# Mask matmuls of two max banks together behind two score units, and PSUM banks split three and three

## The chip, the cores and the metric

The kernel runs on one core of a Trainium2 chip. The metric is the time of one execution in microseconds of device time, lower is better.

## The reference

One transformer layer on x of 16 sequences x 512 tokens x 128 channels: attention with 16 heads of 8 channels, a linear position bias and a causal mask, a residual with a layer norm, then eight experts of which each token takes two, a shared expert, and again a residual with a layer norm.

```python
q = (x @ q_w + q_b)   # 16 heads of 8
att = einsum('bhqd,bhkd->bhqk', q, k) / sqrt(8) + slope[h] * (j - i)
att = softmax(where(causal, att, -inf))
y = einsum('bhqk,bhkd->bhqd', att, v) @ o_w + o_b
x = layernorm(x + y)
x = layernorm(x + shared(x) + routed_top2(x))
```

## The kernel before

The first function, `attention`, does the attention and the first norm; the second, `experts`, the rest. Only the first is touched.

All of a sequence's q and k lie in stacks of bf16 rows: a float is split into three bf16 parts, whose products are summed by stacking them along the contraction, 48 rows, four more for the position bias, and then three rows for the negated row maxima and seven for the cut of blocks above the diagonal. Two heads lie above each other, one in partitions 0 to 63 and one in 64 to 127, so their matmuls use one half of TensorE's rows each.

Four heads make a quad (g = 0 to 3), and a sequence has four quads. The lower triangle of a quad's scores is packed into ten **units** of 512 columns, one PSUM bank each (`scores`, `unit`, L464). Before softmax the row maxima are needed. They come from a **max pass** one or two sequences ahead: 40 banks a sequence (`maxed`, `max_bank`, L441), each the scores without maxima, plus a mask matmul (L461) that adds the causal mask by multiplying an identity of 128 rows with a constant. The mask matmul is 128 columns wide in banks 0 to 3 of ten, 256 in 4 to 7, 384 in 8 and 9. VectorE reduces a bank to its maxima (`take_max`, L724, L732) and frees it by `max_taken`. Max bank n of a group of ten is issued right behind unit n of some quad (`MAX_AT`: quad 0 carries max 10 to 19, quad 1 20 to 29, quad 2 30 to 39, quad 3 0 to 9 of a later sequence), and its head is the neighbour (m ^ 1) of the unit's, so it lies in the other half of the rows and both run side by side.

After each unit: ScalarE takes the exponential (L562, `exp_done` frees the score bank), GpSimd zeroes above the diagonal (L602), and a quad later four matmul groups `pv0` to `pv3` (`weighted`, L482, L493) multiply the probabilities with v in 32-column strips of TensorE, in PSUM bank `pv`; ScalarE copies the result to `yraw` after `pv3` (L517).

Between them stand **jobs**, each a short pipeline through TensorE (all in the single PSUM bank `misc`, in fixed order, see `ready`), ScalarE, VectorE and GpSimd: `xt`, `q`, `k`, `qr`, `kr` (transposed input, q and k and their bf16 parts for the sequence two ahead), `y0` to `y3`, `v`, `yn`, `o`, `ln`, `x1t`, `lg` (normalisation, output projection, layer norm and router logits of the sequence before), `m`, `mr` (row maxima of the next sequence, split in three parts; SyncE then writes them into the stack by six DMAs, L379, which unit 0 and unit 1 of the next sequence wait for). `qr`, `kr`, `ln` and `mr` have no part on TensorE.

The order is one list, `plan(g)` (L164), which every engine walks in its own program, each taking the items that have a part for it. An engine works strictly in that order, so whatever waits holds all behind it. Before, the list is built from fractions of a quad and comes out as follows (max numbers shown from 0):

```
g0: u0 max0 xt u1 max1 pv0 u2 max2 q u3 max3 u4 max4 k pv1 u5 max5 u6 max6 qr pv2 u7 max7 pv3 u8 max8 kr u9 max9
g1: u0 max0 y0 u1 max1 pv0 u2 max2 y1 u3 max3 u4 max4 y2 pv1 u5 max5 u6 max6 y3 pv2 u7 max7 pv3 u8 max8 v u9 max9
g2: u0 max0 u1 max1 yn pv0 u2 max2 u3 max3 o u4 max4 pv1 u5 max5 u6 max6 ln pv2 u7 max7 pv3 u8 max8 x1t u9 max9
g3: u0 max0 u1 max1 m pv0 u2 max2 u3 max3 mr u4 max4 pv1 u5 max5 u6 max6 pv2 u7 max7 pv3 u8 max8 lg u9 max9
```

PSUM has eight banks: two for `scores` (SB), four for `maxed` (MB), `pv` and `misc`. A unit waits for the exponential of the unit SB before it, a max matmul for the reduction of the one MB before it.

Of the kernel before, what the change touches and what calls it, by code (L numbers as in the profile page):

```python
# [12 lines left out]
ACT = mybir.ActivationFunctionType  # L13
# [10 lines left out]
SB, MB = 2, 4  # L24
# [71 lines left out]
def max_stage(n):  # L96

    return 2 if n < 10 else 1
# [65 lines left out]
def plan(g):  # L164

    score = "unit0 unit1 pv0 unit2 unit3 unit4 pv1 unit5 unit6 pv2 unit7 pv3 unit8 unit9".split()
    jobs = list(JOBS[g])
    keyed, units = [], 0
    for x in score:
        if x.startswith("unit"):  # L170
            keyed += [(units / 10, 2, x), (units / 10, 3, f"max{MAX_AT[g] + units}")]
            units += 1
        else:
            keyed.append((units / 10, 1, x))
    early = {"m": 0.2, "mr": 0.35} if g == 3 else {}
    keyed += [(early.get(x, (n + 0.5) / len(jobs)), 0, x) for n, x in enumerate(jobs)]
    in_order = []
    for at, rank, x in sorted(keyed, key=lambda item: (-(-item[0] * 10 // 1), item[1])):
        in_order.append(x)
    return in_order  # L180
# [38 lines left out]
def attention(nc, io, dram, keep):  # L219

    with ExitStack() as ctx:
# [80 lines left out]
        with nc.Block() as block:  # L302
# [84 lines left out]
            def _(pe):  # L387
# [53 lines left out]
                def max_bank(st, n):  # L441
# [11 lines left out]
                    bank = maxed[n % MB]  # L453
                    q, ks = qstack[st.stack(off)], kstack[st.stack(off)]
                    blocks = max_blocks(n)
                    for h, i, col in blocks:
                        rows, slot = rows_of(h, MAX_ROW)
                        pe.matmul(bank[:, col:col + (i + 1) * P], q[rows, slot, i * P:(i + 1) * P],  # L458
                                  ks[rows, slot, 0:(i + 1) * P], start=True, stop=False, skip_group_check=True)
                    at, mask = ((3 * P, slice(0, P)), (2 * P, slice(0, 2 * P)), (P, slice(P, T)))[n % 10 // QUAD]  # L460
# [3 lines left out]
                def unit(st, g, u):  # L464
# [7 lines left out]
                    for hh in range(QUAD):  # L472
                        for kt in range(QT):
                            at, col, width = segment(hh, kt)
                            if at == u:
                                rows, slot = rows_of(g * QUAD + hh, ROWS)
                                last = pe.matmul(scores[n % SB][:, col:col + width],  # L477
# [21 lines left out]
                def body(st):  # L499
                    for g in range(NQUAD):  # L500
                        off, pg = (0, g - 1) if g else (-1, NQUAD - 1)
                        for item in plan(g):
# [4 lines left out]
                            elif item.startswith("max") and st.has(max_stage(int(item[3:]))):  # L507
                                max_bank(st, int(item[3:]))
                            elif item in READERS and st.has(STAGE[item]):
                                job(st, item)  # L510
# [4 lines left out]
            def _(act):  # L515
# [36 lines left out]
                def body(st):  # L552
                    for g in range(NQUAD):
                        off, pg = (0, g - 1) if g else (-1, NQUAD - 1)
                        for item in plan(g):
                            if item.startswith("unit") and st.has(0):
                                u = int(item[4:])
                                act.wait_ge(S["unit_ready"], st.at(0, SEQ_UNITS, UNITS * g + u + 1))
                                if u == 0 and (g >= 2 or not st.first(0)):
# [3 lines left out]
                                               scores[(UNITS * g + u) % SB][:], ACT.Exp).then_inc(S["exp_done"], 1)  # L563
# [67 lines left out]
            def _(dve):  # L631
# [92 lines left out]
                def take_max(st, n):  # L724
# [7 lines left out]
                    dve.tensor_reduce(out.rearrange("p a b -> p (a b)"), maxed[n % MB][:].rearrange("p (j t) -> p j t", t=P),  # L732
# [654 lines left out]
```

## Time and profile before

| | |
|---|---|
| time, median of three runs | 1538.52 us (1532.29 to 1545.63) |
| the profiled execution | 1540.48 us, span 1538.4 us |
| TensorE (PE) busy | 1215.7 us, 79% of the span, 9059 instructions |
| VectorE (DVE) | 857.5 us, 56% |
| ScalarE (ACT) | 771.2 us, 50% |
| GpSimd (POOL) | 609.4 us, 40% |
| mask matmuls (L461) | 640, 179.8 us busy; 151.4 us of idle time before their weight loads |
| mean granted TensorE clock | 0.889 |

Times count from the span's start. "Busy" of an engine is the union of its instructions; a row's idle time and the name behind the arrow say how long the engine stood before it and what ended that. PEld is TensorE's weight loading, which overlaps PE. In a timeline, equal instructions that follow each other are merged into one row with their count.

### The profile page before, as it was taken

Reading aid. Unit: us, or ns where it says so; the run is one execution under the profiler, and the core shown is the slowest. Engines: PE = TensorE matmul, PEld = TensorE weight load, DVE = VectorE, ACT = ScalarE, POOL = GpSimd, SP = SyncE. Lnnn points to the kernel's source line nnn. Section 1 sums busy time; section 2 is a strip of 40 time slices with the busy share of each in tenths; the row PEclk is TensorE's granted clock in tenths of the full one; section 3 lists DMA queues with packets and bytes.
Section 4 is the critical chain, followed back from the end, with each engine's and each line's share of the span. In section 5 each row is a group of like instructions: output and inputs, shape, how many; then the busy total and the mean of one; then the engine's idle time right before and its main releaser. Section 6 shows DMA issues by size and latency. Waiting matters only on the chain. (4 is left out here: it accounts for less than half of the span.)

```text
span 1538.4 us, 29410 instructions
## 1 busy us (share of the span) xinstructions
PE 1215.7 (79%) x9059; PEld 753.4 (49%) x9060; DVE 857.5 (56%) x2153; ACT 771.2 (50%) x1659; POOL 609.4 (40%) x1064
## 2 busy tenths in 40 slices
PE   1989999999999999999864101169799989999865
PEld 0223333333333333333223100069799979999755
DVE  1768888888788888887115000024433325564556
ACT  1036666666666666666621000036566656666332
POOL 0024444444444444444322777600000015552677
PEclk9969999999899999999855555579899989999898
DMA  6433333444323334441106111100022223332222
GB/s 94 59 47 67 67 63 63 61 70 72 73 43 65 65 64 65 63 65 25 32 0 160 55 53 53 48 19 23 28 60 60 60 59 99 103 103 80 70 78 74
DMA packets 147325, 96.41 MB, mean 63 GB/s; under 512 B 21777, under 2 KB 142929, under 8 KB 147026
## 3 DMA queue, kind: packets, MB, share of 16 engines
q1 hardware_dynamic: 131682, 73.19, 24.7%
q0 software_dynamic: 8192, 16.79, 3.8%
q10 hardware_dynamic: 7344, 5.08, 1.4%
q8 instruction: 58, 0.95, 0.3%
q14 instruction: 49, 0.40, 0.1%
HBM read 33.39 MB, written 31.46 MB: 42 GB/s over the span
## 5 line engine op out<-in xcount | busy, mean ns | idle before, releaser
L562 ACT ACTIVATE probs<-scores 128x512 f32<-128x512 f32 x640 | 363.4, 594 | 176.4 <-PE scores L477 176.1
L602 POOL TENSOR_SCALAR_AFFINE_SELECT probs<-probs 128x256 f32<-128x256 f32 (+1 forms) x640 | 241.5, 384 | 360.9 <-ACT probs L562 353.5
L458 PE MATMUL maxed<-kstack,qstack 52*128 52x512 bf16 (+3 forms) x1024 | 261.5, 317 | 30.9 <-DMA kstack<-parts 27.9
L477 PE MATMUL scores<-qstack,kstack 64*128 64x128 bf16 (+3 forms) x1024 | 250.4, 311 | 30.3 <-ACT probs L562 17.9
L1024 DVE TENSOR_TENSOR e_hid<-e_gate,e_up_ps 128x352 f32<-128x352 f32 x208 | 108.2, 520 | 276.0 <-ACT e_gate L1282 184.6
L1205 PE MATMUL e_gate_ps<-e_w_in,e_xT 128*128 (+1 forms) x624 | 164.3, 373 | 91.1 <-issue 73.4
L732 DVE TENSOR_REDUCE maxA<-maxed 128x4 f32<-128x512 f32 x256 | 170.1, 685 | 83.6 <-PE maxed L461 79.9
L493 PE MATMUL pv<-probs,vaug 128*32 128x512 f32 (+3 forms) x2048 | 203.2, 472 | 0.0
L1282 ACT ACTIVATE e_gate<-e_gate_ps 128x352 f32<-128x352 f32 x208 | 96.7, 465 | 201.9 <-PE e_gate_ps L1205 79.2
L732 DVE TENSOR_REDUCE maxB<-maxed 128x4 f32<-128x512 f32 x256 | 168.5, 683 | 28.0 <-PE maxed L461 26.3
L477 PEld LDWEIGHTS scores<-qstack,kstack 64*128 64x128 bf16 x1024 | 65.4, 94 | 234.5 <-ACT probs L562 146.8
L461 PE MATMUL maxed<-causal,identb 128*128 128x128 bf16 (+2 forms) x640 | 179.8, 281 | 0.0
L1323 POOL DMA_INDIRECT e_raw_down<-y_sorted,e_place_best x64 | 63.3, 989 | 289.7 <-DMA y_sorted<-e_raw_down 277.8
L1205 PEld LDWEIGHTS e_gate_ps<-e_w_in,e_xT 128*128 128x128 f32 x624 | 101.6, 198 | 108.0 <-issue 85.1
L1205 PE MATMUL e_up_ps<-e_w_in,e_xT 128*128 (+1 forms) x624 | 141.0, 336 | 0.0
L461 PEld LDWEIGHTS maxed<-causal,identb 128*128 128x128 bf16 x640 | 61.6, 96 | 151.4 <-issue 151.4
L1223 PE MATMUL e_h_ps<-e_ident,e_hid 128*128 128x128 f32 x624 | 106.7, 281 | 21.7 <-issue 15.8
L1234 PE MATMUL e_y_ps<-e_w_down,e_running 128*128 (+3 forms) x624 | 89.7, 281 | 34.7 <-issue 20.5
L1234 PE MATMUL e_y_ps<-e_w_down,e_counts 128*128 (+3 forms) x624 | 89.5, 280 | 32.5 <-issue 31.3
L1205 PEld LDWEIGHTS e_up_ps<-e_w_in,e_xT 128*128 128x128 f32 x624 | 112.7, 200 | 0.0
L1285 ACT ACTIVATE e_xT<-e_x_ps 128x128 fp32r<-128x128 f32 x208 | 57.8, 278 | 92.6 <-remote 31.2
L732 DVE TENSOR_REDUCE maxC<-maxed 128x4 f32<-128x512 f32 x128 | 87.6, 686 | 26.3 <-PE maxed L461 24.6
(158 smaller groups left out, 1737.0 us busy)
## 6 DMA issues: line engine op xcount, KB each, us to landing
qstack<-parts SPq DMA_DIRECT2D x192, 64.0 KB
kstack<-parts SPq DMA_DIRECT2D x192, 64.0 KB
x_sorted<-zeros SPq DMA_DIRECT2D x32, 288.0 KB, 5.3
e_xs<-x_sorted SPq DMA_DIRECT2D x144, 64.0 KB
y_sorted<-e_raw_down SPq DMA_DIRECT2D x144, 64.0 KB, 1.6
xin<-in_x SPq DMA_DIRECT2D x16, 256.0 KB, 3.2
xres<-in_x SPq DMA_DIRECT2D x16, 256.0 KB, 3.3
e_xs<-x_all SPq DMA_DIRECT2D x64, 64.0 KB
```

Of the source, the lines that this page charges most:

```text
L458: pe.matmul(bank[:, col:col + (i + 1) * P], q[rows, slot, i * P:(i + 1) * P], ks[rows, slot, 0:(i + 1) * P], start=True, stop=False, skip_ ...
L461: pe.matmul(bank[:, at:T], identb[:], causal[:, mask], start=False, stop=True, skip_group_check=True).then_inc(S["max_ready"], 1)
L477: last = pe.matmul(scores[n % SB][:, col:col + width], ks[rows, slot, kt * P:(kt + 1) * P], q[rows, slot, kt * P:T], start=True, stop=True)
L493: last = pe.matmul(pv[hh * VW:(hh + 1) * VW, kt * P:T], vaug[st.par(off)][:, kt, g * QUAD + hh, :], probs[g % 2][:, at * T + col:at * T + ...
L562: act.activation(probs[g % 2][:, u * T:(u + 1) * T], scores[(UNITS * g + u) % SB][:], ACT.Exp).then_inc(S["exp_done"], 1)
L602: pool.affine_select(out=view, in_=view, compare_op=ALU.is_ge, fill=0.0, base=0, pattern=pattern, channel_multiplier=-1).then_inc(S["maske ...
L732: dve.tensor_reduce(out.rearrange("p a b -> p (a b)"), maxed[n % MB][:].rearrange("p (j t) -> p j t", t=P), AX.X, ALU.max).then_inc(S["max ...
L1024: dve.tensor_tensor(hid[k][:, 0:F], gate[k][:], up_ps[k][:, 0:F], ALU.mult).then_inc(S["hid_done"], 1)
L1205: last = pe.matmul(bank[:, 0:F], xT[k][:, x_part, :], w_in[:, e, w, w_part, :].rearrange("p a f -> p (a f)"), start=n == 0, stop=n == 2)
L1223: last = pe.transpose(h_ps[:, j * P:(j + 1) * P], hid[k][:, j * P:(j + 1) * P], ident[:])
L1234: last = pe.matmul(y_ps[:, 0:C], hT[k][0:fw, j * P:(j + 1) * P], w_down[0:fw, e, j, :].rearrange("p a c -> p (a c)"), start=j == 0, stop=j ...
L1282: act.activation(gate[k][:], gate_ps[k][:, 0:F], ACT.Silu).then_inc(S["silu_done"], 1)
```

## The change

SB and MB go from 2 and 4 to 3 and 3. The mask matmul leaves `max_bank` for a function of its own, `mask_bank`, and a plan item `mask<n>` issues it for max banks n and n+1. `plan` becomes an explicit loop over pairs of units: unit, max, unit, max, the two masks, a `pv`, a job. As 40 is no multiple of 3, the bank's number now comes from a count over all sequences.

```diff
-SB, MB = 2, 4
+SB, MB = 3, 3
 def plan(g):
...
+    in_order = []
     jobs = list(JOBS[g])
+    after = {0: jobs[0:1], 1: jobs[1:2], 2: jobs[2:3], 3: jobs[3:4], 4: jobs[4:]}
+    if g == 2:
+        after = {0: ["yn"], 1: ["o"], 2: [], 3: ["ln"], 4: ["x1t"]}
+    elif g == 3:
+        after = {0: ["m"], 1: ["mr"], 2: [], 3: ["lg"], 4: []}
+    for n in range(UNITS // 2):
+        for u in (2 * n, 2 * n + 1):
+            in_order += [f"unit{u}", f"max{MAX_AT[g] + u}"]
+        in_order.append(f"mask{MAX_AT[g] + 2 * n}")
+        if n < QUAD:
+            in_order.append(f"pv{n}")
+        in_order += after[n]
     return in_order
 def max_bank(st, n):
-                    bank = maxed[n % MB]
+                    bank = maxed[st.at(off, MAXB, n) % MB]
+                def mask_bank(st, n):
+                    bank = maxed[st.at(max_stage(n), MAXB, n) % MB]
                     at, mask = ((3 * P, slice(0, P)), (2 * P, slice(0, 2 * P)), (P, slice(P, T)))[n % 10 // QUAD]
                     pe.matmul(bank[:, at:T], identb[:], causal[:, mask], start=False, stop=True,
                               skip_group_check=True).then_inc(S["max_ready"], 1)
 def unit(st, g, u):
-                                last = pe.matmul(scores[n % SB][:, col:col + width],
+                                last = pe.matmul(scores[st.at(0, SEQ_UNITS, n) % SB][:, col:col + width],
 def body(st):
+                            elif item.startswith("mask") and st.has(max_stage(int(item[4:]))):
+                                mask_bank(st, int(item[4:]))
+                                mask_bank(st, int(item[4:]) + 1)
```

ScalarE's exponential and VectorE's reduction take their bank's number in the same way. The new lists, with max numbers from 0 and `masks` for two mask matmuls:

```
g0: u0 max0 u1 max1 masks pv0 xt u2 max2 u3 max3 masks pv1 q u4 max4 u5 max5 masks pv2 k u6 max6 u7 max7 masks pv3 qr u8 max8 u9 max9 masks kr
g1: the same with y0, y1, y2, y3, v
g2: the same with yn, o, nothing, ln, x1t
g3: the same with m, mr, nothing, lg, nothing
```

## Rows read from the trace of the kernel before

**Rows 1.** Busy by stretch: from:to, length, PE, PEld, DVE, ACT, POOL, clock, DMA share.
```profile
91.00:742.00 651.00, 607.06 (x5191) 244.94 (x5190) 523.65 (x1106) 426.97 (x788) 299.75 (x685) 0.98 0.37 61
```

**Rows 2.** Timeline of ScalarE: start, length, what; the copies after `pv3`.
```profile
380.14 0.60 ACT L517 ACTIVATE yraw<-pv 128x512 f32<-128x512 f32 x1 [0.22 <-PE pv L493]
393.20 0.60 ACT L517 ACTIVATE yraw<-pv 128x512 f32<-128x512 f32 x1 [0.22 <-PE pv L493]
...
437.76 0.60 ACT L517 ACTIVATE yraw<-pv 128x512 f32<-128x512 f32 x1 [0.23 <-PE pv L493]
...
480.87 0.60 ACT L517 ACTIVATE yraw<-pv 128x512 f32<-128x512 f32 x1 [0.22 <-PE pv L493]
```

**Rows 3.** Waits of one period, 439.6 to 482.7: total us, times, longest.
```profile
PE misc L392 <- DVE x_tiles L717: 1.0, 1, 1.0
...
PE scores L477 <- ACT probs L562: 0.8, 2, 0.5
...
PE scores L477 <- DVE maxA L732: 0.5, 1, 0.5
```

**Rows 4.** Timeline of TensorE in quad 0 (L392 `xt`, L405 `q`).
```profile
440.00 0.61 PE L392 MATMUL misc<-ident,xin 128*128 128x128 f32 x4
440.54 0.39 PE L477 MATMUL scores<-qstack,kstack 64*128 64x512 bf16 x1
...
440.86 0.23 PE L461 MATMUL maxed<-causal,identb 128*128 128x128 bf16 x1
441.02 1.07 PE L493 MATMUL pv<-probs,vaug 128*32 128x512 f32 x8
...
442.34 0.23 PE L461 MATMUL maxed<-causal,identb 128*128 128x128 bf16 x1
442.40 1.08 PE L405 MATMUL misc<-xT,wq 128*128 128x512 f32 x2
...
443.74 0.23 PE L461 MATMUL maxed<-causal,identb 128*128 128x128 bf16 x1
443.90 0.33 PE L477 MATMUL scores<-qstack,kstack 64*128 64x384 bf16 x1
...
444.07 0.22 PE L477 MATMUL scores<-qstack,kstack 64*128 64x128 bf16 x1
```

**Rows 5.** Timeline of TensorE, the same quad: `pv1` and `pv2`.
```profile
445.38 0.85 PE L493 MATMUL pv<-probs,vaug 128*32 128x384 f32 x8
...
447.25 0.43 PE L493 MATMUL pv<-probs,vaug 128*32 128x128 f32 x8
```

**Rows 6.** Timeline of VectorE and ScalarE around `k` (its TensorE part ends 445.38).
```profile
445.49 0.75 DVE L652 TENSOR_SCALAR k_whole<-misc,kb 128x512 f32<-128x512 f32 x1
...
446.28 0.63 ACT L517 ACTIVATE parts<-k_whole 128x512 bf16<-128x512 f32 x1 [0.37 <-DVE k_whole L652]
...
446.81 1.07 ACT L562 ACTIVATE probs<-scores 128x512 f32<-128x512 f32 x2
```

**Rows 7.** Timeline of VectorE in quad 2: job `o`, reductions, `ln`.
```profile
466.54 0.69 DVE L705 TENSOR_TENSOR x_tiles<-misc,xres 128x512 f32<-128x512 f32 x1
...
468.57 1.85 DVE L732 TENSOR_REDUCE maxB<-maxed 128x4 f32<-128x512 f32 x3
470.35 1.49 DVE L717 TENSOR_SCALAR x_tiles<-x_tiles,mean_var,rstd 128x128 f32<-128x128 f32 x4
```

**Rows 8.** Timeline around the DMAs of the row maxima (L379) and unit 1.
```profile
434.80 3.76 SPq L379 DMA_DIRECT2D qstack<-mparts  x6
...
477.57 0.31 DVE L683 TENSOR_TENSOR mparts<-mrest,mparts 64x128 bf16<-64x128 f32 x1
...
477.91 4.53 SPq L379 DMA_DIRECT2D qstack<-mparts  x6
...
483.81 0.09 PEld L477 LDWEIGHTS scores<-qstack,kstack 64*128 64x128 bf16 x1 [0.34 <-DMA qstack<-mparts]
```

**Rows 9.** Busy by stretch, columns as in the first group: a stretch at falling clock.
```profile
380.00:390.00 10.00, 8.65 (x52) 2.42 (x48) 7.67 (x19) 5.47 (x11) 4.16 (x12) 0.70 0.05 14
```

More of the change, by code:

```diff
@@ L164, in plan @@
 def plan(g):
-    score = "unit0 unit1 pv0 unit2 unit3 unit4 pv1 unit5 unit6 pv2 unit7 pv3 unit8 unit9".split()
+    in_order = []
     jobs = list(JOBS[g])
[L168 to L179, printed above, removed]
+    after = {0: jobs[0:1], 1: jobs[1:2], 2: jobs[2:3], 3: jobs[3:4], 4: jobs[4:]}
[10 more added lines that the diff above has]
+        in_order += after[n]
     return in_order
@@ L452, in max_bank @@
                         pe.wait_ge(S["max_taken"], st.at(off, MAXB, n - MB + 1))
-                    bank = maxed[n % MB]
+                    bank = maxed[st.at(off, MAXB, n) % MB]
                     q, ks = qstack[st.stack(off)], kstack[st.stack(off)]
-                    blocks = max_blocks(n)
-                    for h, i, col in blocks:
+                    for h, i, col in max_blocks(n):
                         rows, slot = rows_of(h, MAX_ROW)
@@ L562, in body @@
                                 act.activation(probs[g % 2][:, u * T:(u + 1) * T],
-                                               scores[(UNITS * g + u) % SB][:], ACT.Exp).then_inc(S["exp_done"], 1)
+                                               scores[st.at(0, SEQ_UNITS, UNITS * g + u) % SB][:], ACT.Exp).then_inc(S["exp_done"], 1)
                             elif item == "pv3" and st.has(off):
@@ L731, in take_max @@
                         out = maxC[:, h:h + 2, :]
-                    dve.tensor_reduce(out.rearrange("p a b -> p (a b)"), maxed[n % MB][:].rearrange("p (j t) -> p j t", t=P),
+                    dve.tensor_reduce(out.rearrange("p a b -> p (a b)"), maxed[st.at(max_stage(n), MAXB, n) % MB][:].rearrange("p (j t) -> p j t", t=P),
                                       AX.X, ALU.max).then_inc(S["max_taken"], 1)
```

## Prediction

> **What bounds the kernel now.** I read the busy time by stretch first [rows 1]. From 91 to 742 us all sixteen sequences pass through attention; TensorE is busy 607 of 651 us (93%), VectorE 524 (80%), ScalarE 427 (66%). Nothing behind attention uses the plan or the banks, so only this stretch can change, and I read it for one sequence. The copies of `yraw` after `pv3` repeat exactly: from the one at 437.76 to the one four quads on, at 480.87, is 43.1 us [rows 2]; some 14.5 such periods carry the whole max pass (the last sequence has none left to do). The list of waits of one period [rows 3] shows what TensorE misses: 1.0 us for the normalised tile before `x1t`, 0.8 us for exponentials, 0.5 us for a reduction; with 93% busy that is about 3 us of 43.1 in all. So TensorE is the bound, by a small margin.
>
> Its own timeline [rows 4] shows what it spends. Below, a time from one row to the next is the difference of starts. A score and a max matmul of 512 columns run side by side (on the two halves of the rows). From 440.54 to the mask at 440.86 is 0.32 us, though 512 columns at the granted 2.4 GHz take 0.21: about 0.10 us more before a full-height matmul may start. From a 128-column mask (0.05 us of columns) to the next unit is 0.16 (443.74 to 443.90), to `pv` 0.16, but to `q`, which is full-height too, only 0.06. So a change of shape (half-height rows, full height, 32-column strips) costs about 0.10 us each time, and a repeat costs none: the second segment of a unit follows after 0.17 us, the length of its 384-column predecessor (443.90 to 444.07).
>
> The Trainium skill, TensorEngine Tiling (Array Packing), Key Properties, says that changing the tiling mode, not just the tile, drains TensorE; that is the gap seen above. The Trainium skill, TensorE: Matmul & The Clock Gate, Part 3, The mechanism, adds that a weight load overlaps running matmuls only where the row group differs; by that rule a second unit behind the first would show its load of 0.09 us [rows 8] and 20 pairs would lose 1.8 us of the 2.9 saved below. The 0.17 us spacing on one row group speaks against it here.
>
> **Part 1: masks in pairs.** Counting changes of shape through the old plan gives 24 a quad (10 from a unit into a mask, 10 into a unit, 4 into `pv`; jobs stand behind masks and cost none), 96 a sequence. The new one has 5 + 5 + 4 and one for each job that now stands behind a `pv` (3, 4, 2 and 2): 17, 18, 16 and 16, 67 in all. That is 29 fewer at 0.10, so 2.9 us of TensorE time per sequence, 42 us in 14.5. If nothing else became late this would be the gain. A step that no row shows is `pv` straight into a full-height job (11 a sequence): between 0 and 0.2 us (twice the dearest change seen), taken as 0.1 like the others. Unit after unit is also unseen: between 0.22 (columns alone, as within a unit) and 0.32 (with a drain); I take 0.22.
>
> **Part 2: later masks, three max banks, later jobs.** A max bank 2k+1 now needs the reduction of 2k-2, the first of the pair just before; with four banks there was one more in between. A job waits behind its `pv`. I follow one sequence in five legs, each from its latest chain. u is a unit, g0 to g3 the quads.
>
> Leg A, g0 u1 to the end of `k`: TensorE alone. Units 0.32 + 0.54 + 0.55, mask pairs 0.23 + 0.23 + 0.33 (0.07 or 0.11 for the first, 0.16 or 0.21 for the second), `pv0` 1.00, `pv1` 0.78, `pv2` 0.36 [rows 4, 5] (a row's duration overlaps its follower by 0.07, which is taken off), `xt` 0.54, `q` and `k` 1.02 each. Sum 6.9.
>
> Leg B, end of `k` to g1 u1: ScalarE. After `k` VectorE starts 0.11 later and takes 0.75; ScalarE's `k` copy 0.05 later, its follower 0.54 after that; two exponentials 1.07 [rows 6]; `yraw` copy 0.5; the `qr` copy, now behind it, 0.54; the exponential of unit 8 0.6, and 0.1 back to TensorE, where u1, three banks on, waits for it. Sum 4.2. TensorE's own work there is 2.7 (four units 1.1, masks 0.33 and 0.44, `pv3` 0.57, u0 0.22), so it stands 1.5 us even with three score banks; before, the exponentials cost it 0.8 [rows 3].
>
> Leg C, g1 u1 to the end of `o` in g2: TensorE again. Fourteen units in pairs, their masks, two `pv0` and two `pv1`, one `pv2`, one `pv3` (0.57, midway between its neighbours), five transpose jobs at 0.54 like `xt`, `v` and `o` 1.0 each (estimates from `q`). Sum 14.8. VectorE has 14 reductions at 0.60 there (their pace when they queue, three in 1.85 [rows 7]), 8.4 us, and jobs under 3 us: hidden.
>
> Leg D, end of `o` to g3 u0: VectorE. The `o` job (add, statistics) runs from 466.54 to 468.57, 2.03 us [rows 7]; behind it now stand four reductions (max 34 to 37) in place of three, 0.60 each, then `ln` 1.49, then `x1t` 0.54: with 0.1 to 0.2 at each hand-over 6.9 us, 0.6 of it new. TensorE reaches max 37 after 1.46 (u4 and u5 0.55, masks 0.33, `pv2` 0.36, u6 0.22), but the reduction of max 34, queued behind the `o` job, ends at 2.8: it waits 1.4 us there, and the masks of 36 and 37, `pv3` and u8 are late behind it; then `x1t` waits 1.3 us for `ln`. TensorE's savings of this leg go entirely into these two waits.
>
> Leg E, g3 u0 to g0 u1: the DMA of the row maxima. `m` now follows `pv0`: 0.54 + 0.23 + 1.00 + 0.20 = 2.0; the next pair's masks stand at 2.5, two reductions follow, and the `mr` job starts at 4.0 after u0. From its start to the unit that reads the result the trace has 477.57 to 483.81, 6.2 us, with a wait for the DMA already shown [rows 8]; there the six issues take 4.53, elsewhere 3.76, which makes 5.5. So u1 comes 9.5 to 10.2 after g3 u0; 9.8 taken. TensorE alone would be there after 8.3 (ten units 2.7, masks 1.6, the four `pv` 2.7, `m` and `lg` 1.1, u0 0.2).
>
> Sum: 6.9 + 4.2 + 14.8 + 6.9 + 9.8 = 42.6 us, against 43.1. Of 2.9 us saved some 0.5 is left; the rest becomes waiting.
>
> The other moves are hidden: ScalarE's, GpSimd's and SyncE's parts of `q` and `k` (24 stack DMAs) come up to two units later, but their stack is first read in g3, two quads on; GpSimd is busy 300 of 651 us [rows 1], and `pv` needs its selects a quad later.
>
> **Score banks 2 to 3** show in leg B: u9 and the next u0 may stand three exponentials ahead instead of two. They cost nothing but the max bank they take.
>
> **Sum.** 14.5 periods times 0.45 is 6.5 us. The start (max pass alone, 42 to 91 us) and the last sequence have the same chains of jobs; I take zero, give or take 3. Against that one more stretch at half clock: between the copies at 380.14 and 393.20 a quad took 13.1 us [rows 2] at a mean clock of 0.70 over ten of them [rows 9], where a quarter of the period is 10.8; TensorE's idle time grows from 3 to about 6 us a sequence, so I add 1. The profiled execution took 1540.5 us around a span of 1538.4; that gives 1535, and since it stood 2 above the median of the three runs (1538.5), 1533.
>
> **Rivals.**
>
> *The waits dissolve.* Where TensorE runs ahead, VectorE and ScalarE get their work earlier and may catch up; if leg E's DMA wait or leg B's exponential wait (1.5 us each) is absorbed, a period is 41.1: 1511; both, 39.6: 1490. For it: 2.9 us is a count on rows. Against: each leg's chain consists of durations, not of queues. From 0.7 us absorbed per period on it decides. Chance 0.28, around 1510.
>
> *The clock falls.* The new idle time is bunched (1.5 us before g1 u1, 1.4 and 1.3 in leg D). In the profile it fell without one long gap [rows 9]. The price is 13.1 less 10.8, 2.3 us; in every second sequence that gives 17 us, 1549, in each one 33 us, 1565. From about nine sequences on it ends slower. Chance 0.13. The Trainium skill, TensorE: Matmul & The Clock Gate, "A second HAM failure mode: psum-queue depth-cycling", tells of just this, micro-idle pieces at bank turns that make the clock oscillate; the trace agrees, with 0.70 in that stretch.
>
> *The pairs do not save.* If unit after unit costs 0.32, legs A and C grow by 0.1 for each of 11 pairs, 1.1 us: 1549. If `pv` into a job costs 0.2 as well, 9 of these add 0.9: 1562. Against: the repeat within a unit is free. Chance 0.14.
>
> **How the numbers follow.** Forecast 0.45, dissolve 0.28, clock 0.13, no saving 0.14. About 1% is what a measurement of this kernel tells from no change, 1523 to 1554. Faster: 0.28. Slower: the clock 0.13 and 0.09 of the last, 0.22. Same: the rest, 0.50. The range 1504 to 1562 leaves out both waits dissolved (below) and the clock falling in every sequence (above).
>
> **What would show it.** The idle time ahead of the masks' weight loads falls by about half. The period stands at 42.6 instead of 43.1. Score matmuls wait for the DMA of the maxima in nearly every sequence, about 1.5 us. Max matmul 37 waits for a reduction, `x1t` for `ln` about 1.3 us; the exponential before g1 u1 is waited for 1.5 us. A period at or under 41.4 would show legs B or E wrong; one above 43.6, the unit spacing or the clock.

## The result and the profile after

| | before | changed |
|---|---|---|
| median of 14 runs each | 1539.85 us (1531.42 to 1546.67) | 1520.21 us (1506.05 to 1527.88) |
| ratio, 95% interval | | 0.986 (0.9836 to 0.9883) |
| profiled execution, span | 1540.48, 1538.4 | 1506.05, 1504.0 |
| last copy of `yraw` (end of attention) | 789.10 | 758.93 |

The changed kernel is 1.4% faster. The forecast was 1533 us, with "no change" (1523 to 1554) as the likeliest class. The time lies in the range, 12.8 us below the forecast, but just under the 1523 that the prediction set as the edge of "no change", and the interval of the ratio leaves out 1. The profiled execution is the fastest of its 14, 14 us under their median, so terms read from it are compared with a second profile of each kernel below. Of all executions of this case two count as slow and stand in no ratio: one of the single masks (2546.56 us) and one of the jobs ahead of `pv` (1367.67).

Most lines moved down by three to six: scores are L480, max matmuls L457, masks L464, `pv` L496, exponentials L568, reductions L738, the copies to `yraw` L523, `ln` L723.

Busy by stretch, columns as in [rows 1], changed kernel, over the sequences that carry a max pass:

```profile
91.00:680.00 589.00, 533.97 (x4844) 221.12 (x4844) 494.21 (x1039) 383.58 (x735) 278.56 (x636) 0.99 0.40 66
```

TensorE is busy 91%, VectorE 84%. In the kernel before the same instructions take 91 to 698 us, and the shares are 94% and 82% ([rows 1] runs on to 742 us, into quads without max pass). TensorE lost work and VectorE came closer to it. The period, by the copies to `yraw` as in [rows 2] (timeline of ScalarE, changed kernel):

```profile
382.63 0.60 ACT L523 ACTIVATE yraw<-pv 128x512 f32<-128x512 f32 x1 [0.23 <-PE pv L496]
394.95 0.60 ACT L523 ACTIVATE yraw<-pv 128x512 f32<-128x512 f32 x1
404.35 0.60 ACT L523 ACTIVATE yraw<-pv 128x512 f32<-128x512 f32 x1
415.85 0.60 ACT L523 ACTIVATE yraw<-pv 128x512 f32<-128x512 f32 x1 [1.47 <-PE pv L496]
424.84 0.60 ACT L523 ACTIVATE yraw<-pv 128x512 f32<-128x512 f32 x1 [0.23 <-PE pv L496]
```

From 382.63 to 424.84 it is 42.2 us, where 43.1 was before and 42.6 forecast. What TensorE waits for in it (waits of 384.9 to 427.1; columns as in [rows 3]):

```profile
PE scores L480 <- ACT probs L568: 1.1, 2, 0.8
PE misc L392 <- DVE x_tiles L723: 1.0, 1, 1.0
PE maxed L457 <- DVE maxB L738: 1.0, 1, 1.0
PE scores L480 <- DMA qstack<-mparts: 0.7, 1, 0.7
```

These are the four waits that the prediction named, each at its place, and each smaller than forecast: 0.8 us before g1 u1 (the larger of the two in the first row) where it had 1.5, 1.0 for 1.3, 1.0 for 1.4, and 0.7 for 1.5. On TensorE's timeline of the same period:

```profile
385.57 0.39 PE L480 MATMUL scores<-qstack,kstack 64*128 64x512 bf16 x1 [0.71 <-DMA qstack<-mparts]
...
387.69 0.39 PE L480 MATMUL scores<-qstack,kstack 64*128 64x512 bf16 x1
387.70 0.60 PE L457 MATMUL maxed<-kstack,qstack 52*128 52x512 bf16 x2
387.92 0.38 PE L480 MATMUL scores<-qstack,kstack 64*128 64x512 bf16 x1
388.23 0.29 PE L464 MATMUL maxed<-causal,identb 128*128 128x128 bf16 x2
388.45 0.85 PE L496 MATMUL pv<-probs,vaug 128*32 128x384 f32 x8
389.23 1.12 PE L405 MATMUL misc<-xT,wq 128*128 128x512 f32 x2
...
392.57 0.33 PE L480 MATMUL scores<-qstack,kstack 64*128 64x384 bf16 x1
...
396.61 0.39 PE L480 MATMUL scores<-qstack,kstack 64*128 64x512 bf16 x1 [0.83 <-ACT probs L568]
...
414.50 0.39 PE L457 MATMUL maxed<-kstack,qstack 52*128 52x384 bf16 x2 [1.01 <-DVE maxB L738]
...
417.79 0.63 PE L392 MATMUL misc<-ident,x_tiles 128*128 128x128 f32 x4 [1.02 <-DVE x_tiles L723]
```

Unit follows unit after 387.92 − 387.69 = 0.23 us, the columns alone (so in five of the six pairs of 512 columns of this period in which no wait stands; the sixth has 0.33). The pair of masks starts 0.31 behind the second unit, and `pv1` stands 0.22 behind it. From `pv1` to `q` it is 0.78, what the prediction took for `pv1` ahead of a unit, so a `pv` into a job is as dear as one into a unit. A pair does save TensorE its changes of shape. In the sum it is less than was counted: from copy to copy TensorE is busy 40.4 of 43.1 us before (437.76 to 480.87) and 38.4 of 42.2 now (382.63 to 424.84), 2.0 us less where the count has 2.9, and its idle time grew from 2.7 to 3.8. The idle time ahead of the masks' weight loads fell, in 100 to 680 us, from 118.2 (534 recorded) to 74.0 us (552): 37% less, not the half that was forecast (weight loads of the changed kernel, 100 to 680 us: busy, mean ns of one, then idle and its cause):

```profile
L464 PEld LDWEIGHTS maxed<-causal,identb 128*128 128x128 bf16 x552 | 31.4, 97 | 74.0 <-issue 74.0
```

**Where the 32 us between the profiles lie.** A second profile of each kernel, on one chip, gives spans of 1538.5 and 1506.6. Divided by the copies to `yraw`, the second pair and in brackets the first:

| stretch | before | changed | less |
|---|---|---|---|
| up to the copy in g1 of the second sequence | 155.2 (153.5) | 147.6 (148.5) | 7.6 (5.0) |
| the twelve periods from there | 525.9 (523.9) | 514.2 (511.9) | 11.7 (12.0) |
| two quads more | 20.7 (20.7) | 20.5 (20.5) | 0.2 (0.2) |
| the last nine quads | 89.7 (91.0) | 76.3 (78.0) | 13.4 (13.0) |

Of the twelve periods' gain 12 x 0.9 = 10.8 is the period. Quads that stand above the others, at a low clock or behind a late DMA, come on top and nearly cancel: before they are five in the second pair (11.91, 13.07, 11.86, 11.86 and 11.85 us where the others take 10.4), 8.6 us in all, in the changed kernel chiefly three (13.86, 13.82 and 16.02 against 12.32), 7.6 us in all. Of the last nine quads it is chiefly the last five, in which nothing of the max pass runs any more, that gain: 50.9 us before and 39.1 changed (50.5 and 39.3). Behind attention the second pair is equal, 747.0 and 748.0. So some 11 of the 32 us are the period, and more than half of the gain came from the first sequence and from the end of attention. The max pass alone (42 to 91 us), ahead of the first sequence, gained nothing: ScalarE's first `xT` copy behind it comes at 93.67 us before and 93.63 changed (93.05 and 94.45 in the first pair). In the first sequence the granted clock is 0.68 from 93 to 116 us before and 0.80 from 93 to 110 changed; why it stays low for less time no run here takes apart.

Busy by stretch of the last five quads before (cut at the copies to `yraw`; after the length PE, PEld, DVE, ACT, POOL, clock, DMA share):

```profile
738.60:750.50 11.90, 9.28 (x58) 2.60 (x58) 0.19 (x1) 6.17 (x12) 3.95 (x11) 0.66 0.33 76
750.50:761.10 10.60, 9.73 (x65) 3.48 (x62) 2.19 (x8) 6.09 (x11) 4.54 (x11) 0.74 0.00 0
761.10:769.30 8.20, 7.07 (x62) 2.86 (x60) 1.94 (x9) 6.64 (x14) 3.25 (x9) 1.00 0.12 35
769.30:781.80 12.50, 9.03 (x53) 2.05 (x52) 1.50 (x4) 6.59 (x12) 5.83 (x16) 0.65 0.00 0
781.80:789.10 7.30, 7.23 (x44) 3.29 (x42) 0.19 (x1) 1.70 (x3) 2.18 (x4) 0.50 0.00 0
```

and changed:

```profile
719.60:730.60 11.00, 8.39 (x59) 2.36 (x58) 0.19 (x1) 5.95 (x13) 3.65 (x11) 0.69 0.35 84
730.60:738.10 7.50, 6.81 (x61) 2.82 (x60) 1.64 (x6) 5.74 (x13) 4.85 (x12) 1.00 0.00 0
738.10:745.70 7.60, 7.12 (x66) 2.96 (x64) 2.49 (x11) 6.07 (x14) 2.62 (x9) 1.00 0.04 11
745.70:755.50 9.80, 6.96 (x53) 2.07 (x52) 1.49 (x4) 6.20 (x14) 6.07 (x16) 0.83 0.07 21
755.50:758.90 3.40, 3.37 (x42) 1.53 (x42) 0.19 (x1) 1.70 (x4) 2.15 (x5) 1.00 0.00 0
```

The clock column shows the difference. Without max pass TensorE has only ten units, `pv` and jobs a quad. Before, it stood for an exponential six times (3.9 us in 740 to 789), and its clock was 0.50 to 0.74 in four of the five stretches; the same matmuls (the last stretch, 42 to 44 of them) take 7.23 us at a granted 0.50 and 3.37 at 1.00. Changed, it stood for an exponential twice (1.1 us), and the clock was full in three of five, though its waits for `ln` and the DMA grew from 3.6 to 5.4 us.

**The clock in the changed kernel.** The mean of 0.99 hides short falls, in the twelve periods at 172 and 514 us in the first profile and at 172, 342 and 513 in the second. From g3's copy to g0's these quads take 13.87 and 14.73 us, and 13.86, 13.82 and 16.02, where the others take 12.32. Each fall lies at TensorE's wait for the DMA of the maxima, of 0.7 us in three of them and of 1.3 in the two at 513 and 514. Here is the first, by stretch and on TensorE's timeline (the `pv0` takes 1.93 us where it takes 1.06 elsewhere):

```profile
169.01:182.88 13.87, 12.93 (x98) 4.82 (x98) 8.93 (x15) 7.47 (x14) 3.34 (x10) 0.88 0.19 54
```

```profile
171.95 0.39 PE L480 MATMUL scores<-qstack,kstack 64*128 64x512 bf16 x1 [0.72 <-DMA qstack<-mparts]
...
172.49 1.93 PE L496 MATMUL pv<-probs,vaug 128*32 128x512 f32 x8
```

### The profile page after: what moved, and what is told of

The parts are those of the page before. It is cut to its first block and busy times, and to the rows that moved or that the text cites. A ratio compares the mean times of both kernels' runs of the same rounds, so it can differ in the third digit from the quotient of the medians.

```text
span 1504.0 us, 29409 instructions
## 1 busy us (share of the span) xinstructions
PE 1161.2 (77%) x9058; PEld 737.1 (49%) x9060; DVE 855.8 (57%) x2153; ACT 752.5 (50%) x1659; POOL 606.7 (40%) x1064
## 5 line engine op out<-in xcount | busy, mean ns | idle before, releaser
L568 ACT ACTIVATE probs<-scores 128x512 f32<-128x512 f32 x640 | 344.6, 596 | 109.0 <-PE scores L480 103.8
L457 PE MATMUL maxed<-kstack,qstack 52*128 52x512 bf16 (+3 forms) x1024 | 219.6, 313 | 50.1 <-DMA kstack<-parts 28.4
L480 PE MATMUL scores<-qstack,kstack 64*128 64x128 bf16 (+3 forms) x1024 | 204.8, 304 | 32.9 <-DMA qstack<-mparts 16.3
L738 DVE TENSOR_REDUCE maxA<-maxed 128x4 f32<-128x512 f32 x256 | 164.5, 684 | 78.5 <-PE maxed L464 74.8
L496 PE MATMUL pv<-probs,vaug 128*32 128x512 f32 (+3 forms) x2048 | 197.0, 458 | 0.0
L738 DVE TENSOR_REDUCE maxB<-maxed 128x4 f32<-128x512 f32 x256 | 164.5, 684 | 13.3 <-PE maxed L464 7.3
L480 PEld LDWEIGHTS scores<-qstack,kstack 64*128 64x128 bf16 x1024 | 68.0, 95 | 151.9 <-ACT probs L568 69.2
L464 PE MATMUL maxed<-causal,identb 128*128 128x128 bf16 (+2 forms) x640 | 123.3, 276 | 0.0
L457 PEld LDWEIGHTS maxed<-kstack,qstack 52*128 52x128 bf16 x1024 | 67.3, 95 | 80.8 <-issue 39.8
L1240 PEld LDWEIGHTS e_y_ps<-e_w_down,e_counts 128*128 128x128 f32 (+1 forms) x624 | 79.9, 196 | 33.0 <-issue 32.9
```

What stands on the lines that cost most here:

```text
L464: pe.matmul(bank[:, at:T], identb[:], causal[:, mask], start=False, stop=True, skip_group_check=True).then_inc(S["max_ready"], 1)
L480: last = pe.matmul(scores[st.at(0, SEQ_UNITS, n) % SB][:, col:col + width], ks[rows, slot, kt * P:(kt + 1) * P], q[rows, slot, kt * P:T], ...
L496: last = pe.matmul(pv[hh * VW:(hh + 1) * VW, kt * P:T], vaug[st.par(off)][:, kt, g * QUAD + hh, :], probs[g % 2][:, at * T + col:at * T + ...
L568: act.activation(probs[g % 2][:, u * T:(u + 1) * T], scores[st.at(0, SEQ_UNITS, UNITS * g + u) % SB][:], ACT.Exp).then_inc(S["exp_done"], 1)
L738: dve.tensor_reduce(out.rearrange("p a b -> p (a b)"), maxed[st.at(max_stage(n), MAXB, n) % MB][:].rearrange("p (j t) -> p j t", t=P), AX. ...
L1240: last = pe.matmul(y_ps[:, 0:C], hT[k][0:fw, j * P:(j + 1) * P], w_down[0:fw, e, j, :].rearrange("p a c -> p (a c)"), start=j == 0, stop=j ...
```

## Experiments

Three chips served the experiments. On one of them, that of the first four (single masks, banks three and three, banks two and four, jobs ahead of `pv`), everything behind attention takes about 175 us less, and the kernel before has a median of 1368.42. Attention takes the same: with banks three and three, which ran on two chips, it ends at 756.3 and 754.8. So each kernel is compared with the kernel before on its own chip. As the same saving is a larger share of 1368 us than of 1540, it is also given in us, as the difference of the medians. The periods are read as above from the copies to `yraw`.

| kernel | ratio, 95% interval | saved, us | period, us | last copy of `yraw` |
|---|---|---|---|---|
| before | | | 43.1 | 789.1, 791.5 |
| changed | 0.986 (0.9836 to 0.9883) | 19.6 | 42.2 | 758.9 |
| changed, again | 0.984 (0.9763 to 0.9917) | 28.1 | 42.2 | 758.6 |
| changed, single masks | 0.996 (0.9933 to 0.9988) | 6.4 | 43.8 | 779.6 |
| before, banks 3 and 3 | 0.973 (0.9678 to 0.9777) | 35.2 | 41.9 | 756.3 |
| before, banks 3 and 3, on another chip | 0.978 (0.9732 to 0.983) | 34.1 | 41.9 | 754.8 |
| changed, banks 2 and 4 | 0.998 (0.9952 to 1.0016) | 1.7 | 44.1 | 783.0 |
| changed, jobs ahead of `pv` | 0.984 (0.9773 to 0.9898) | 21.5 | 43.6 and 42.05 | 765.8 |
| old order, pairs, banks 3 and 3 | 0.974 (0.9664 to 0.9819) | 44.2 | 41.45 | 744.7 |
| jobs ahead of `pv`, `qr`, `kr` later | 0.979 (0.9712 to 0.987) | 36.8 | 41.7 | 748.6 |
| changed, `o`, `m` ahead of `pv` | 0.987 (0.9827 to 0.9907) | 21.6 | 41.85 | 758.9 |
| old order, pairs but in front of `qr`, `kr` | 0.977 (0.9734 to 0.981) | 35.7 | 41.15 | 745.7 |

### The change taken apart: masks, banks, order

**Single masks** in the new order, with three and three banks:

```diff
-            in_order += [f"unit{u}", f"max{MAX_AT[g] + u}"]
-        in_order.append(f"mask{MAX_AT[g] + 2 * n}")
+            in_order += [f"unit{u}", f"max{MAX_AT[g] + u}", f"mask{MAX_AT[g] + u}"]
...
                                 mask_bank(st, int(item[4:]))
-                                mask_bank(st, int(item[4:]) + 1)
```

> The changed kernel with the mask matmul put back right behind its own max matmul; order of jobs and the 3 + 3 banks stay. Theory (changes of shape cost 0.10 us each): 40 more of them per sequence than in the changed kernel, 107 against 67, so 4.0 us more TensorE work per sequence; banks are released earlier, so up to 1.5 us of its waits (1.0 for max 37, part of the exponentials) go: a period of 44 to 46 us where the changed kernel has 42.2, and a ratio to the kernel before of 1.01 to 1.03. Rival (the gain came from the order or the banks, not from pairing): period near 42.2, ratio 0.98 to 0.99.

The period is 43.8 us, 1.6 above the changed kernel. Counted as in the prediction, this kernel has 24 changes of shape a quad and one more for each of the 11 jobs that stand behind a `pv`, 107 a sequence, against 67: 4.0 us of TensorE time saved by the pairs. By its busy time (41.9 of 43.8 us here, 38.4 of 42.2 in the changed kernel) it is 3.5, and 1.6 reach the period; the rest is idle time.

**Banks three and three alone**, old order, single masks:

```diff
-SB, MB = 2, 4
+SB, MB = 3, 3
...
-                    bank = maxed[n % MB]
+                    bank = maxed[st.at(off, MAXB, n) % MB]
```

and the same count over sequences in the three other places where a bank is chosen.

> The kernel before with only the banks changed to 3 for scores and 3 for the max pass, masks and order as before. Theory: the waits for exponentials before u9 and the next u0 (0.8 us a period) go, waits for a reduction behind the o job come (up to 1 us); period 42.8 to 43.4 us, ratio 0.995 to 1.005. Rival (the score bank is what gained): period 42.2 to 42.4, ratio 0.98 to 0.99.

This single line of meaning does at least as well as the whole change. It saves 35.2 us, 34.1 when it ran again, where the changed kernel saves 19.6 and 28.1. Both its intervals lie below that of the changed kernel's first ratio, but they overlap that of its second, and no chip ran both kernels side by side; in the profiles its attention ends only 2 to 4 us earlier. The period is 41.9. The waits of one period, kernel before (384 to 427, its second profile):

```profile
PE misc L392 <- DVE x_tiles L717: 1.0, 1, 1.0
...
PE scores L477 <- ACT probs L562: 0.8, 2, 0.5
...
PE scores L477 <- DVE maxA L732: 0.5, 1, 0.5
```

and with banks three and three (384 to 426):

```profile
PE misc L392 <- DVE x_tiles L717: 0.9, 1, 0.9
...
PE misc L392 <- issue: 0.4, 1, 0.4
```

The 1.3 us that units waited are gone, and all of it was waiting for exponentials. The third row names a reduction, but in the program a unit waits for no reduction: the reduction only ended last, and the weight load of the same matmul names the exponential (timeline of the kernel before, first profile, where it is the unit at 452.36):

```profile
452.35 0.09 PEld L477 LDWEIGHTS scores<-qstack,kstack 64*128 64x128 bf16 x1 [0.71 <-ACT probs L562]
```

In the period the fourth max bank bought nothing that three do not. By quads, nearly all of it lies between the copies of g0 and g1, 10.41 us before and 9.32 now.

At the end of attention it is less clear. The last five quads take 50.5 and 50.9 us before. With three score banks they take 37.4 to 39.5 us in nine profiles of eight kernels, this one among them with 38.1. But its second profile, on the other chip, has 43.8, with a granted clock of 0.67, 0.71 and 0.67 in three of the five. And 44.2 is what the new order and the pairs reach with two score banks (below). So the third score bank alone gave 12.6 and 6.9 us there, and order and pairs alone 6.5; the 11 to 12 us of the changed kernel can't be put down to one of them.

**The changed kernel with banks two and four:**

```diff
-SB, MB = 3, 3
+SB, MB = 2, 4
```

> The changed kernel with the banks back at 2 for scores and 4 for the max pass. Theory: leg D is bound by VectorE's chain behind o, so without the 1.0 us wait of max 37 the wait of x1t for ln grows by as much and nothing is gained; with two score banks the unit before g1 u1 waits for an exponential one later, 0.5 us more; period 42.5 to 43.0, ratio 0.99 to 0.997. Rival (the third max bank's absence costs its full 1.0 us): period 41.2 to 41.7, ratio under 0.983.

Ratio 0.998: without the third score bank the new order and the pairs give nothing in the whole. They lose in the period what they gain in the first sequence (the copy in g1 of the second sequence at 146.75 us, where the kernel before has 153.5 and 155.2) and in the last nine quads (81.8 us against 91.0 and 89.7). The period, 44.1, is partly the clock. TensorE waits once 1.78 us for `ln`, then (busy by stretch):

```profile
372.00:382.00 10.00, 8.60 (x82) 3.58 (x81) 8.37 (x24) 6.18 (x12) 4.42 (x12) 1.00 0.69 118
382.00:387.00 5.00, 4.62 (x24) 1.18 (x25) 3.41 (x10) 2.06 (x5) 1.35 (x4) 0.66 0.01 3
```

The wait before this fall, on TensorE's timeline:

```profile
382.38 0.69 PE L392 MATMUL misc<-ident,x_tiles 128*128 128x128 f32 x4 [1.78 <-DVE x_tiles L723]
```

So it is in twelve of thirteen sequences. The one without the fall has 10.14 us in that quad instead of 11.66, a period of 42.6. With the falls left out the third score bank thus brings 0.4 us in the new order, where TensorE's waits lie elsewhere, and 1.2 in the old.

**The account of the period:** banks −1.2 (43.1 to 41.9), new order +1.9 (41.9 to 43.8), pairs −1.6 (43.8 to 42.2), together −0.9. This holds along this path only: the parts act on each other, as the 0.4 just above and the 0.5 to 0.8 that pairs save in the old order (below) show. The order that the change introduces to make room for pairs costs more than pairs bring in it. Of the 1.9 us, 1.4 are busy time of TensorE (40.6 to 41.9), where the count of shapes has 1.1 for the 11 jobs behind a `pv`; the rest is waiting.

**Both kernels again**, together on one chip, on which the kernel before takes what it took in the result:

> The changed kernel itself once more, on the chip of these runs. It should show the same period of 42.2 us and the same four waits (0.2 and 0.8 for an exponential, 1.0 for a reduction, 1.0 for ln, 0.7 or more for the DMA). Theory: of its gain 13 us come from 14.5 periods of 0.9 us, the rest from the last sequence, whose quads ran at half clock or not by chance in the two profiles; then the attention's end varies by some 10 us from run to run and the ratio is 0.98 to 0.99. Rival (the last sequence gains for a reason of the change): the end of attention is within 3 us of 759 again, and the ratio is under 0.98.

> The kernel before once more, for its profile on this chip: period 43.1 us. Theory (half clock in the last sequence is chance): attention ends between 775 and 792. Rival: at 789 within 2 us, since two score banks let the clock fall there each time.

The ratio was found again, 0.984; the two profiles are those of the division above. The theory of both expectations, that half clock in the last sequence is chance and moves the end of attention by some 10 us, was not borne out: it ended at 791.5 against 789.1, and at 758.6 against 758.9. The ratio is the one that the theory gave.

### What in the order costs: the jobs behind `pv`

**Jobs ahead of `pv`:**

```diff
         in_order.append(f"mask{MAX_AT[g] + 2 * n}")
+        in_order += after[n]
         if n < QUAD:
             in_order.append(f"pv{n}")
-        in_order += after[n]
```

> The changed kernel with each job put ahead of its pv instead of behind it. Theory: the 11 changes from pv into a full-height job go (11 x 0.10 = 1.1 us a sequence), m comes 1.0 us earlier, so the wait for the DMA of the maxima (0.7 to 1.3 us) nearly goes, o comes 0.8 us earlier against the same work of VectorE behind it; period 40.0 to 41.0 us where the changed kernel has 42.2, ratio to the kernel before 0.965 to 0.975. Rival (jobs need their place behind pv to find VectorE and ScalarE ready): new waits before the jobs of 0.5 us or more each, period at or above 42.2, ratio 0.985 or more.

No gain that the intervals tell, and the distance from g0's to g1's copy is 10.60 to 10.66 us in nine of thirteen sequences (the next expectation says ten of fourteen) and 9.08 in the other four. In the nine there is one wait for an exponential, then low clock (TensorE's timeline, then busy by stretch):

```profile
400.41 0.39 PE L480 MATMUL scores<-qstack,kstack 64*128 64x512 bf16 x1 [1.60 <-ACT probs L568]
```

```profile
389.00:400.40 11.40, 9.51 (x82) 3.24 (x82) 9.13 (x15) 7.26 (x15) 4.26 (x10) 1.00 0.32 82
400.40:404.60 4.20, 4.19 (x22) 1.25 (x23) 2.42 (x5) 2.35 (x5) 4.08 (x7) 0.59 0.57 78
```

Without the falls its period would be 42.05, 0.2 under the changed kernel. TensorE is busy 37.2 us in it, 1.2 less than in the changed kernel, as the count has it for 11 changes of shape fewer (1.1): the bound in this order is mostly the chains, not TensorE.

**`qr` and `kr` later**, on top of the jobs ahead of `pv`, so that ScalarE has its exponentials first (`qr` behind unit 9, `kr` in quad 1):

```diff
+    if g == 0:
+        after = {0: ["xt"], 1: ["q"], 2: ["k"], 3: [], 4: ["qr"]}
+    elif g == 1:
+        after = {0: ["y0"], 1: ["kr", "y1"], 2: ["y2"], 3: ["y3"], 4: ["v"]}
...
+        in_order += after[n]
         if n < QUAD:
             in_order.append(f"pv{n}")
-        in_order += after[n]
```

> Masks in pairs and jobs ahead of pv as in the run with jobs first, with qr moved behind unit 9 and kr into quad 1. Theory: the wait of g1 u1 for the exponential of unit 8 (1.6 us there), which stands behind ScalarE's qr copy, goes, and with it the fall of the clock that followed it in 10 of 14 sequences (1.5 us each): a period of 40.2 to 41.0 us against 43.6 or 42.05 there; ratio 0.957 to 0.970. Rival (the clock falls behind the other waits too, or ScalarE is late elsewhere): the period stays at or over 41.8.

41.7 us, and of the falls between the copies of g0 and g1 none is left (one other, at 506 us, remains). So the 1.6 us wait and the falls after it went together, and the cause was ScalarE's `qr` and `kr` copies between exponentials. What the order still costs shows in waits that the changed kernel lacks or has smaller: for `ynorm` 0.7, for `vaug` and `rowmax` 0.3 each, and 0.9 for the DMA of the maxima.

**Only `o` and `m` ahead of `pv`**, since they start the chains of legs D and E:

```diff
+        first = [x for x in after[n] if x in ("o", "m")]
+        in_order += first
         if n < QUAD:
             in_order.append(f"pv{n}")
-        in_order += after[n]
+        in_order += [x for x in after[n] if x not in first]
```

> The changed kernel with only two jobs moved: o ahead of pv1 in quad 2 and m ahead of pv0 in quad 3; the rest stay behind their pv. Theory (what the new order costs lies in VectorE's chain behind o and in the DMA chain behind m, which both begin one pv later than before): the leg that ends with o gets 0.8 us shorter with the leg behind it unchanged, and the wait for the DMA (0.7 to 1.3 us) shrinks or goes: a period of 40.6 to 41.5 us against 42.2. Rival (the cost of the order lies in q and k): 42.0 us or more.

0.35 us of the 1.9, and the time is the changed kernel's (0.987). What the period gained the clock took: six of thirteen sequences have a quad of 13.9 to 15.0 us where 12.3 is the usual length, at a mean granted clock of 0.88, behind the wait for the DMA; the changed kernel has two and three such quads. That wait stays 0.71 us though `m` came earlier, so `mr`, which did not move, would set it. The remainder of the 1.9 I could not put to one job; it stays open.

### Pairs in the old order

**Old order, banks three and three**, a mask held back until two wait or until a job or a `pv` comes that TensorE must run:

```diff
...
+        if len(waiting) == 2 or waiting and not x.startswith(("unit", "max")) and x not in ("qr", "kr", "ln", "mr"):
+            in_order += waiting
+            waiting = []
         in_order.append(x)
+        if x.startswith("max"):
+            waiting.append("mask" + x[3:])
...
```

> The old order of units, jobs and pv with the 3 + 3 banks, and masks paired only where two units stand side by side in that order (24 changes of shape fewer than before: 72 against 96). Theory: the new order costs 1.9 us a period (the run with single masks in the new order 43.8, the run with the old order and 3 + 3 banks 41.9), the pairing saves; so 41.9 less at most 2.4: 39.8 to 41.2 us, ratio 0.955 to 0.970. Rival (pairing itself delays reductions so that it only pays in the new order): 41.7 to 42.5 us, ratio 0.973 to 0.985.

41.45 us, 0.46 under the banks alone. The plan has 11 pairs, so 22 changes of shape are saved (96 to 74; the expectation counted 24), 2.2 us by the count and 1.7 by TensorE's busy time (40.6 to 38.9). g0 got slower by 0.4. There two pairs hold back the masks of a max bank until just ahead of `qr` and behind `kr`, which have no TensorE part but stand in VectorE's and ScalarE's programs among the reductions and exponentials. The first unit of g1 then waits 0.64 us. As above its matmul names the reduction that ended last, and its weight load the exponential that it waited for (timelines of both):

```profile
390.50 0.09 PEld L487 LDWEIGHTS scores<-qstack,kstack 64*128 64x128 bf16 x1 [1.03 <-ACT probs L574]
...
390.51 0.39 PE L487 MATMUL scores<-qstack,kstack 64*128 64x512 bf16 x1 [0.64 <-DVE maxC L744]
```

**The same without the pairs at `qr` and `kr`:**

```diff
-        if len(waiting) == 2 or waiting and not x.startswith(("unit", "max")) and x not in ("qr", "kr", "ln", "mr"):
+        if len(waiting) == 2 or waiting and (g == 0 and waiting[0] == "mask15" or not x.startswith(("unit", "max")) and x not in ("ln", "mr")):
```

> The old order with 3 + 3 banks and pairs, without the two pairs of quad 0 that stand ahead of qr and kr (masks 15 and 16, 18 and 19 single). Theory: in the run with those pairs quad 0 took 12.4 us where the run with single masks takes 12.0, as the later mask holds VectorE's qr part, then ScalarE's copy and exponentials, for which u0 of quad 1 waits 0.64 us; the other quads keep their 0.2, 0.2 and 0.4 us of gain: a period of 41.0 to 41.2 us against 41.45. Rival: the lateness comes from masks 13 and 14 ahead of k, and the period stays at 41.4 or more.

41.15 us, as expected from the chain. In the time it did not show (0.977): the profile has quads of 12.13, 12.14 and 11.28 us, where 9.8 is the usual length.

**Banks alone, again**, beside it:

> The banks alone once more, to stand on one chip with the two others: period 41.9 us, attention ends near 756; a ratio to the kernel before of 0.972 to 0.98 on either chip, so under the changed kernel's 0.984 to 0.986. Rival (the lead of the banks alone came with that chip): 0.985 or more.

0.978 here, 0.973 on the other chip, 34 and 35 us saved. The intervals of both kernels with pairs in the old order (0.974 and 0.977) overlap these. So the times don't tell that pairs add to the banks, though in the profiles attention ends some 10 us earlier with them (744.7 and 745.7 against 756.3 and 754.8). The pairs in the old order beat the changed kernel where both ran on one chip (1494.53 to 1503.71 us against 1509.34 to 1517.02). The simplest version that does as well as the change is the kernel before with banks three and three.

## Why the prediction was right and wrong

**TensorE is the bound, by a small margin:** right. 94% became 91%, VectorE 84%, and half of what TensorE saved turned into waits for ScalarE, VectorE or the DMA (2.0 us less busy, 0.9 off the period).

**A change of shape costs 0.10 us, a repeat none:** right in the rows, 0.23 from unit to unit, and a `pv` into a job costs what a `pv` into a unit does (0.78 for `pv1`). The rival that pairs do not save is refuted by these two rows and by the single masks. In the sum the term was too large: 2.9 us counted, 2.0 measured. A unit lies on the half of the rows on which the max matmul before it has just run, and starts 0.22 us after it (387.92 against 387.70), with its own weight load of 0.09 us between. The Trainium skill, TensorE: Matmul & The Clock Gate, Part 3, The mechanism, says in one place that a weight load overlaps running matmuls only where the row group differs, which the 0.22 contradicts, and in another that it may also go ahead to the background weight buffer, which the 0.22 allows; the measurement decides.

**The five legs.** Measured on TensorE's timeline, forecast in brackets: A 7.00 (6.9), B 4.04 (4.2), C 15.03 (14.8), D 6.71 (6.9), E 9.43 (9.8). Sum 42.21 (42.6). The largest miss is E, 0.37. Its two parts were right: `mr` starts 4.0 us after g3 u0 (forecast 4.0), and from it to u1 it is 5.44 (5.5 for the fast issues). Only the value taken, 9.8 between 9.5 and 10.2, was wrong: the issues went at their fast pace (timeline of the DMA queue's issues):

```profile
422.64 3.77 SPq L379 DMA_DIRECT2D qstack<-mparts  x6
```

In D the reductions were no faster than assumed, but `ln` was.

```profile
413.79 2.64 DVE L738 TENSOR_REDUCE maxB<-maxed 128x4 f32<-128x512 f32 x4
416.35 1.29 DVE L723 TENSOR_SCALAR x_tiles<-x_tiles,mean_var,rstd 128x128 f32<-128x128 f32 x4
```

The fence is VectorE's timeline: four reductions take 2.56 us up to `ln` (forecast 2.4), and `ln` 1.29, where [rows 7] has 1.49. With the period saving 0.9 instead of 0.45, that term is 13 us over 14.5 periods, not 6.5; over the twelve that can be read it is 11.7 and 12.0.

**Score banks, "they cost nothing but the max bank they take" and show in leg B:** the step whose size failed. I counted the third bank as a detail of leg B and never asked what it does by itself. I also misread [rows 3]: "0.5 us for a reduction" was a unit's wait for an exponential too, so two score banks cost 1.3 us a period and not 0.8. In the old order the third bank gives 1.2 us in each period, and 7 to 13 us in the last five quads, where no max pass runs.

**The start and the last sequence, "the same chains of jobs; I take zero, give or take 3":** right for the start, the max pass alone, and wrong for the end, which is the largest miss, 13 us. The prediction read the stretch with max pass and argued by likeness for the one without, where the clock had already fallen to 0.50 to 0.74. One row by stretch of 740 to 789 us would have shown it. The first sequence was counted among the 14.5 periods as one like the others; from the `xT` copy at its beginning to the copy in g1 of the second it gained 6.4 and 7.6 us, where its share of the periods is about 1. With these terms the sum for the profile is 1540.5 − 13 − 13 − 5 = 1510 us, against 1506.05 measured. For the median that sum is too low, 1520.2 was measured. So it is in part luck that the forecast of 1533 is only 12.8 off. The profiled runs of the changed kernel stand 5 and 14 us below the medians of their chips, those of before within 2. The mean granted clock of each of the 14 runs goes with its time: 0.897 and 0.896 in the two fastest, 0.886 and 0.885 in the two slowest. So the slower ones had more time at a low clock; in which stretch no row shows, and this part stays open.

**One more stretch at half clock (+1):** not seen, rather fewer. The changed kernel has two such stretches in its twelve periods in one profile and three in the other, the kernel before three and five.

**The waits dissolve (0.28):** by the time (1510 against 1520.2) this rival came as near as the forecast, but not for its reason. No chain was absorbed, all four waits are there, each 0.3 to 0.8 us smaller than forecast; the period of 42.2 lies between the forecast and its 41.1.

**The clock falls (0.13):** in the changed kernel in two or three of twelve periods, not in every second, and behind the DMA wait, where the prediction did not look for it. In two near variants it fell where it did look: behind single waits of 1.6 us before g1 u1, in nine of thirteen sequences, and of 1.78 us at `x1t`, in twelve of thirteen. The price was 1.5 us a quad, not 2.3.

## What to carry to other kernels

When a change bundles a buffer split with an order, run the split alone first: here it saved by itself at least what the whole change did, and in the period the order cost what the pairs saved. When a row of waits names a releaser that the program has no semaphore for at that place, look at the row of the weight load, or at what else ended in the same 0.1 us. Read the stretches where the bound is another one (the first and last turns of a loop) by their own rows, and look at the granted clock in them before putting them down at zero. A batch of two that holds back another engine's work can give part of its saving back: here 0.3 us of the period came back when the two pairs beside `qr` and `kr` were split.

## What the runs showed of the hardware

- The granted clock fell behind single waits of TensorE, more often behind the long ones. Behind a wait of 1.78 us it fell in twelve of thirteen sequences (0.66 in the 5 us behind it), behind one of 1.60 in nine of thirteen (0.59 in the 4 us behind it). But the same waits stand in the sequences without a fall too. And it also fell behind waits of 0.7 us, in a few sequences of the changed kernel (two falls in one profile, three in the other, two of these five behind 1.3 us) and in six of the variant with `o` and `m` first. So the length of the wait alone does not decide; what else does no run here shows. Matmuls at half clock take double (7.23 against 3.37 us for the last stretch), and a fall cost about 1.5 us in its quad.
- A 64-row matmul follows another on the same half of the rows without a gap (0.22 to 0.23 us for 512 columns, against 0.32 into a full-height mask).
- The same program, banks three and three, took 1333.25 us on one chip and 1505.55 on another, with attention equal (it ends at 756.3 and 754.8). Most of the difference is in the experts' part, in GpSimd's wait ahead of its indirect gathers from the rows that were stored before: 124.4 us of idle time on the one, 288.6 on the other, with the gathers themselves equal (62.8 and 62.9 us):

```profile
L1323 POOL DMA_INDIRECT e_raw_down<-y_sorted,e_place_best x64 | 62.8, 982 | 124.4 <-DMA y_sorted<-e_raw_down 112.5 <-issue 11.9
```

```profile
L1323 POOL DMA_INDIRECT e_raw_down<-y_sorted,e_place_best x64 | 62.9, 982 | 288.6 <-DMA y_sorted<-e_raw_down 276.6 <-issue 12.0
```

Why it differs no run here shows.
